# One-hot rows of destinations made by VectorE instead of ScalarE, and two of 128 gather groups loaded row by row from ScalarE's queue

## The chip, the cores and the metric

The kernel runs on one core of one Trainium2 chip. The metric is the device time of one execution in microseconds (us), lower is better. Five engines work side by side, each through its own queue in order: TensorE (PE; PEld is its weight loads), VectorE (DVE), ScalarE (ACT), GpSimd (POOL) and SyncE (SP). They wait for each other through semaphores. SP, ACT and POOL also issue DMA transfers.

## The reference

One graph attention layer with a residual and a layer norm. There are 12500 nodes of 96 features, 8 heads of 12, and 412500 edges, sorted by destination:

```
Q, K, V = x @ Wq + bq, x @ Wk + bk, x @ Wv + bv          # per node
E       = edge_attr @ We + be                            # per edge
score   = exp(clip(sum_head(K[src] * Q[dst] / sqrt(12) * E), -5, 5))
wV, Z   = segment_sum(V[src] * score, dst), segment_sum(score, dst)
out     = layernorm(x + wV / (Z + 1e-6))
```

## The kernel before

A first part of some 140 us makes a table of K and V rows and a table of Q rows in HBM, and works out for each chunk of edges its least destination. The main loop then goes over 806 chunks of 512 edges (128 partitions times 4 groups), one chunk a step, in loops unrolled by 32 steps. The last part, some 65 us, turns the sums back, divides, adds x and normalises. All order is written out by hand: each engine has its own list of instructions per step, and semaphores tie the lists.

What each engine does in one step s of the main loop:

- POOL gathers the K and V rows of a chunk's sources, one indirect DMA for each group of 128 edges (L683), into a ring of 16 slots. It may run up to eight chunks ahead of the messages that VectorE has made (the wait for `msg_ready`).
- SP loads edge attributes, query windows and destinations for eight chunks ahead. It also loads one group of one chunk in 32 by single rows.
- ACT waits for the scores of chunk s-1 and takes their exponential twice (L940, L942). Then it makes the one-hot rows `ohT` of chunk s+4 in two passes: `away` = abs(destination - row) (L946), `ohT` = relu(1 - away) (L949). Every fourth step it copies source numbers (L904). Then it loads single rows.
- PE projects the edge attributes (L798), picks the query rows with `ohT` (L803), sums the messages of chunk s-5 (L809) and transposes the edge attributes of chunk s+3 (L820).
- DVE adds the sums of chunk s-5 (L1156), multiplies keys, queries and edges (L1171, L1174), sums per head (L1178). Then it waits for the exponentials of chunk s-1, makes `oh` (L1183) and the messages (L1195). It copies the transposed edge attributes of chunk s+2 out of PSUM (L1202, `eaT`) and clips the scores of chunk s (L1209).

The single rows are in `load_rows`: with `load_row_sources` a list of source numbers (`act_idx`, `sp_idx`) is put on one partition. Then each step reads some entries of the list into registers with one TENSOR_LOAD (L466) and issues one small DMA for each entry (L470):

```
for p0 in range(first, last, ROW_LOAD):          # ROW_LOAD = 10
    count = min(ROW_LOAD, last - p0)
    nodes = nc.values_load_multi_w_load_instructions(idx[0:1, p0:p0 + count], ...)
    for r, node in zip(range(p0, p0 + count), nodes):
        engine.dma_start(rows[...], kv_dram[bass.ds(node, 1), :] ...)
```

ACT does this for one group of the chunk at place 31 of every 32: the list is asked for at place u = 0, and from u = 1 on five rows a step are issued (places 1 to 26). In a loaded step they stand in ACT's queue between the exponentials of one step and those of the next. SP issues 19 rows every four steps, as a list read of ten entries and one of nine.

Of the kernel before, what the change touches and what calls it, by code (L numbers as in the profile page):

```python
# [5 lines left out]
ALU = mybir.AluOpType  # L6
ACT = mybir.ActivationFunctionType
# [7 lines left out]
P = 128  # L15
HEADS = 8
G = 4
CHUNK = P * G
# [4 lines left out]
DEPTH = 4  # L23
TURN_LEAD = 3
COPY_LEAD = 2
Q_DEPTH = 2
TURN_DEPTH = 2
MSG_RING = 8
OUT_RING = 8
TURN_DST = 9  # L30
SEL = WIN * PARTS
SEL_READ = 106
SEL_LOAD = 102
RING = 16
KV_RING = 16
HALF = 4
# [4 lines left out]
BLOCK = 32  # L41
SP_CHUNK = 15
ACT_CHUNK = 31
ACT_GROUPS = 1
SP_STEP = 19
ACT_STEP = 5
ROW_LOAD = 10
IDX_RING = 16
IDX_GROUP = 4
# [39 lines left out]
def gnn_kernel(nc, x, src, dst, edge_attr, Wq, bq, Wk, bk, We, be, Wv, bv, out):  # L89
    N, D = x.shape  # L90
# [4 lines left out]
    C = (E + CHUNK - 1) // CHUNK  # L95
# [23 lines left out]
    with ExitStack() as ctx:  # L119
        def sb(name, shape, dt=F32):  # L120
            return ctx.enter_context(nc.sbuf_tensor(name, shape, dt))

        def sem(name):
            return ctx.enter_context(nc.semaphore(name))
# [7 lines left out]
        part = sb("part", [P, 1])  # L132
        sel_row_i = sb("sel_row_i", [P, 1], I32)
        sel_row = sb("sel_row", [P, 1])
        minus_row = sb("minus_row", [P, 1])
        ident = sb("ident", [P, P])
        w_kvq = sb("w_kvq", [DA, 3 * D])
        w_e = sb("w_e", [DA, D])
# [22 lines left out]
        accT = sb("accT", [P, N_PAD])  # L161
# [12 lines left out]
        most = sb("most", [1, 1], I32)  # L174
        act_idx = sb("act_idx", [1, ACT_GROUPS * P], I32)
        act_rows = sb("act_rows", [P, ACT_GROUPS, 2 * D])
        sp_idx = sb("sp_idx", [1, P], I32)
# [6 lines left out]
        off_b = off_mem[:, :].rearrange("p (c e) -> p c e", e=CHUNK)  # L184
# [4 lines left out]
        away = sb("away", [SEL, 2, CHUNK], BF16)  # L189
        ohT = sb("ohT", [SEL, MSG_RING, CHUNK], BF16)  # L190
# [14 lines left out]
        acc_first = sb("acc_first", [P, 1])  # L205
# [62 lines left out]
        off8_made = sem("off8_made")  # L268
        off8_stored = sem("off8_stored")
        tabs_in = sem("tabs_in")  # L270
        minus_row_set = sem("minus_row_set")
        node_id_ready = sem("node_id_ready")
        dst_turned = sem("dst_turned")
        rel_made = sem("rel_made")
# [1 line left out]
        acc_zeroed = sem("acc_zeroed")  # L276
# [7 lines left out]
        kv_in = [sem(f"kv_in{i}") for i in range(KV_RING)]  # L284
        act_idx_in = sem("act_idx_in")
        act_rows_allowed = sem("act_rows_allowed")
        act_rows_in = [sem(f"act_rows_in{i}") for i in range(2 * ACT_GROUPS)]
        sp_idx_in = sem("sp_idx_in")
        sp_rows_allowed = sem("sp_rows_allowed")
        sp_rows_in = [sem(f"sp_rows_in{i}") for i in range(2)]  # L290
# [1 line left out]
        columns_made = sem("columns_made")  # L292
        ea_flipped = sem("ea_flipped")
        ea_turned = sem("ea_turned")
        away_done = sem("away_done")
        ohT_built = sem("ohT_built")
        kq_done = sem("kq_done")
        kqe_done = sem("kqe_done")
# [53 lines left out]
        def landed_half(engine, c, u):  # L352

            if isinstance(c, int):
                engine.wait_ge(off_b_in[u // HALF], 16 * (c // RING + 1))
            else:
                engine.wait_ge(off_b_in[u // HALF], (c - u) * (16 // RING) + 16)
# [92 lines left out]
        WHOLE = C // BLOCK * BLOCK  # L450
        gathered = {SP_CHUNK: G - 1, ACT_CHUNK: G - ACT_GROUPS}

        def groups_gathered(s, u):

            return G if isinstance(s, int) and s == SP_CHUNK else gathered.get(u, G)
# [21 lines left out]
        block = ctx.enter_context(nc.Block())  # L477
# [397 lines left out]
        def _(act):  # L875
# [24 lines left out]
            def copy_sources(s, u):  # L900

                count = max(0, min(IDX_GROUP, C - s)) if isinstance(s, int) else IDX_GROUP
                if count > 0:
                    nc.scalar.copy(src_idx[:, u:u + count, :], src_tab[:, bass.ds(s * G, count * G)].rearrange(  # L904
                        "p (c g) -> p c g", g=G)).then_inc(src_copied, count)
# [22 lines left out]
            run_batches(act, query_batch, BATCHES, 2, 1)  # L928


            act.wait_ge(minus_row_set, 1)

            wait_all(act, kv_stored)

            def step(s, u, _):

                m, t, w = s - 1, s + DEPTH, (u + DEPTH) % RING
                if not isinstance(s, int) or 0 <= m < C:
                    act.wait_ge(score_ready, m + 1)
                    nc.scalar.activation(msg[:, (u - 1) % MSG_RING, :, D:DZ],  # L940
                                         score[:, (u - 1) % 2, :].rearrange("p (g h) -> p g h", g=G), ACT.Exp)
                    nc.scalar.activation(weight_ps[(u - 1) % DEPTH], score[:, (u - 1) % 2, :], ACT.Exp).then_inc(exp_done, 1)  # L942
                if not isinstance(s, int) or t < C:
                    if w % HALF == 0:
                        landed_half(act, t, w)
                    nc.scalar.activation(away[:, u % 2, :], off_b[0:SEL, w, :], ACT.Abs,  # L946
                                         bias=minus_row[0:SEL, 0:1]).then_inc(away_done, 1)
                    act.wait_ge(away_done, t + 1)
                    nc.scalar.activation(ohT[:, w % MSG_RING, :], away[:, u % 2, :], ACT.Relu, bias=1.0, scale=-1.0).then_inc(ohT_built, 1)  # L949
                    if isinstance(s, int) and s == -1:  # L950
                        nc.scalar.copy(accT[:, N // 2:N], acc_first[:, 0:1].to_broadcast((P, N - N // 2))).then_inc(acc_zeroed, 1)

                if u % IDX_GROUP == 0 and (not isinstance(s, int) or s > 0):
                    copy_sources(s + IDX_AHEAD, (u + IDX_AHEAD) % IDX_RING)
                if not isinstance(s, int) or 0 <= s < WHOLE:
                    first = s - u
                    if u == 0:
                        load_row_sources(act, first + ACT_CHUNK, ACT_GROUPS, act_idx, act_idx_in)
                    if u == 1:

                        act.wait_ge(act_idx_in, first // 2 + 16)
                        act.sem_inc(act_rows_allowed, 1)
                        if not isinstance(first, int) or first > 0:
                            act.wait_ge(msg_ready, first)
                        act.sem_inc(act_rows_allowed, 1)
                    lo, hi = (u - 1) * ACT_STEP, min(u * ACT_STEP, ACT_GROUPS * P)
                    if u >= 1 and lo < hi:
                        load_rows(act, lo, hi, act_idx, act_rows, act_rows_in)
# [39 lines left out]
        def _(dve):  # L1008
# [13 lines left out]
            nc.vector.tensor_scalar(sel_row_i[:, :], sel_row_i[:, :], 9, None, ALU.logical_shift_right).then_inc(ident_step, 1)  # L1022
            dve.wait_ge(ident_step, 3)
            nc.vector.tensor_copy(sel_row[:, :], sel_row_i[:, :]).then_inc(ident_step, 1)
            nc.vector.tensor_scalar(minus_row[:, :], sel_row_i[:, :], -1.0, None, ALU.mult).then_inc(minus_row_set, 1)
            nc.vector.tensor_tensor(ident[:, :], iota[:, :], part[:, 0:1].to_broadcast((P, P)), ALU.is_equal).then_inc(ident_ready, 1)
            dve.wait_ge(w_kvq_in, 16 * 6)
            nc.vector.tensor_scalar(w_kvq[:, 2 * D:3 * D], w_kvq[:, 2 * D:3 * D], QSCALE, None, ALU.mult).then_inc(w_q_scaled, 1)
# [94 lines left out]
            for b in range(BATCHES + 1):  # L1123
                query_batch(b, b % 4)
                k = b - BATCHES // 2
# [8 lines left out]
            def step(s, u, base):  # L1134


                a, m, n = s, s - 1, s - SUM_LAG
# [19 lines left out]
                if scores:  # L1157
                    here, block = groups_gathered(a, u), a // BLOCK if isinstance(a, int) else block_now[0]
                    if u in gathered:

                        before = 0 if u == SP_CHUNK else 16 * gathered[SP_CHUNK]
                        dve.wait_ge(kv_in[ua], block * (16 * sum(gathered.values())) + (before + 16 * gathered[u] + 16))
                    else:
                        landed(dve, kv_in, a, ua, 16 * G, u)
                    if here < G:
                        for rows_in in sp_rows_in if u == SP_CHUNK else act_rows_in:
                            dve.wait_ge(rows_in, block * (8 * P) + (0 if u == SP_CHUNK else 8 * P))
                        rows = sp_rows if u == SP_CHUNK else act_rows
                        nc.vector.tensor_tensor(kqe[:, here:G, :], rows[:, :, 0:D],
                                                q_ps[u % Q_DEPTH][:, here * D:G * D].rearrange("p (g d) -> p g d", g=G - here), ALU.mult)  # L1170
                    nc.vector.tensor_tensor(kqe[:, 0:here, :], kv[:, ua, 0:here, 0:D],  # L1171
                                            q_ps[u % Q_DEPTH][:, 0:here * D].rearrange("p (g d) -> p g d", g=here), ALU.mult).then_inc(kq_done, 1)
                    dve.wait_ge(kq_done, a + 1)
                    nc.vector.tensor_tensor(kqe[:, :, :], kqe[:, :, :],  # L1174
                                            e_ps[v].rearrange("p (g d) -> p g d", g=G), ALU.mult).then_inc(kqe_done, 1)
# [23 lines left out]
                k = s + COPY_LEAD  # L1199
                if not isinstance(s, int) or 0 <= k < C:  # L1200
                    dve.wait_ge(ea_flipped, k + 1)
                    nc.vector.tensor_copy(eaT[0:D, (u + COPY_LEAD) % DEPTH, :], turn_ps[(u + COPY_LEAD) % TURN_DEPTH][0:D, :]).then_inc(ea_turned, 1)  # L1202
                if isinstance(s, int) and s == -1:

                    nc.vector.memset(accT[0:D, 0:N // 2], 0.0)
                    nc.vector.memset(accT[D:P, 0:N // 2], 1e-6).then_inc(acc_zeroed, 1)
# [130 lines left out]
```

## Time and profile before

| | before |
|---|---|
| time, median of 3 runs | 4123.18 us (4119.38 to 4124.28) |
| the profiled execution: time, span | 4121.44 us, 4119.6 us |
| mean granted TensorE clock | 0.509 of full speed |
| busy share of the span: PE, PEld | 87%, 85% |
| busy share: DVE, ACT, POOL | 66%, 34%, 75% |

Busy time counts neither instructions of an engine's sequencer (register reads, waits) nor the issue of DMAs. An engine that is 34% busy can still have a full queue. The span runs from the first to the last instruction; 1.84 us of the execution's time lie outside it.

### The profile page before, as it was taken

The page shows a single profiled execution, that of the slowest core. Times are in us where ns is not written, and L with a number is a line of the kernel's source. Part 1 is how long each engine was busy: PE and PEld are TensorE (multiplying, and loading weights), DVE is VectorE, ACT ScalarE, POOL GpSimd, SP SyncE. Part 2 cuts the span into 40 slices and gives each one's busy share as a digit, 9 for nine tenths or more (in the row PEclk, how much of TensorE's full clock was granted, in tenths as well). Part 3 has the DMA queues.
Part 4 walks back from the last instruction along what each step waited for, and adds up shares of the span by engine and source line. Part 5 has one row for each costly group of instructions (what it writes and reads, how often), then busy time and mean ns, then how long its engine had stood idle before and what let it go on. Part 6 is the DMA issues. An engine that isn't in the chain of part 4 may idle for free.

```text
span 4119.6 us, 87353 instructions
## 1 busy us (share of the span) xinstructions
PE 3603.4 (87%) x20000; PEld 3508.7 (85%) x20001; DVE 2730.4 (66%) x6963; ACT 1402.6 (34%) x3656; POOL 3096.0 (75%) x3312
## 2 busy tenths in 40 slices
PE   7799988888888888888888888888888888888886
PEld 7799988888888888888888888888888888888885
DVE  4777766666666666666666666666666666666667
ACT  3433333333333333333333333333333333333335
POOL 8777777777777777777777777777777777777775
PEclk8555555555555555555555555555555555555555
DMA  8555545444454454444544454444544444444443
GB/s 269 165 142 144 144 136 140 134 133 135 133 141 133 133 138 139 133 133 135 141 134 133 134 139 136 133 134 135 141 133 133 136 141 133 134 135 134 141 124 112
DMA packets 409729, 574.44 MB, mean 139 GB/s; under 512 B 160715, under 2 KB 330476, under 8 KB 409268
## 3 DMA queue, kind: packets, MB, share of 16 engines
q0 software_dynamic: 154480, 316.87, 29.3%
q1 hardware_dynamic: 237361, 239.83, 19.3%
q10 hardware_dynamic: 17426, 13.83, 1.1%
q14 instruction: 446, 3.65, 0.3%
q8 instruction: 16, 0.26, 0.0%
HBM read 547.39 MB, written 22.87 MB: 138 GB/s over the span
## 4 chain that ended last, share of the span: by engine, by line
POOL 53%; issue 20%; DVE 7%; DMA 6%; PE 4%; ACTq 3%; ACT 2%; POOLq 1%; DVEq 1%
POOL kv_mem L683 53%; DMA kv_mem<-kv_table,src_idx 5%; ACTq L470 3%; DVE kqe L1174 1%; PE bank L798 1%; DVE kqe L1171 1%; PE bank L809 1%; DVE msg_mem L1195 1%; ACT away L946 1%; PE bank L820 1%; ACT ohT L949 1%; ACTq L466 1%; DVE eaT L1202 1%; DVE oh L1183 1%; DVE y_stats L1296 0%
## 5 line engine op out<-in xcount | busy, mean ns | idle before, releaser
L683 POOL DMA_INDIRECT kv_mem<-kv_table,src_idx x3175 | 3004.0, 946 | 978.9 <-issue 946.3
L798 PE MATMUL bank<-w_e,eaT 97*128 97x96 f32 x6448 | 1500.1, 414 | 1.9 <-DVE eaT L1202 1.9
L798 PEld LDWEIGHTS bank<-w_e,eaT 97*128 97x128 f32 x6448 | 1474.4, 334 | 10.7 <-DVE eaT L1202 2.1
L820 PE MATMUL bank<-ident,ea_mem 128*96 128x128 f32 x3224 | 868.8, 425 | 450.1 <-DVE eaT L1202 435.6
L809 PE MATMUL bank<-oh,msg_mem 128*104 128x32 f32 x6448 | 1257.9, 360 | 1.9 <-DVE msg_mem L1195 1.9
L809 PEld LDWEIGHTS bank<-oh,msg_mem 128*104 128x104 f32 x6448 | 1211.2, 293 | 2.2 <-DVE msg_mem L1195 2.2
L940 ACT ACTIVATE msg_mem<-score 128x32 f32<-128x32 f32 x806 | 184.8, 229 | 2596.4 <-DVE score L1209 1956.7
L820 PEld LDWEIGHTS bank<-ident,ea_mem 128*96 128x96 f32 x3224 | 569.3, 205 | 518.2 <-DVE eaT L1202 478.0
L1171 DVE TENSOR_TENSOR kqe<-kv_mem,bank 128x384 f32<-128x384 f32 (+1 forms) x806 | 439.6, 545 | 716.1 <-DMA kv_mem<-kv_table,src_idx 711.2
L946 ACT ACTIVATE away<-off_mem,minus_row 96x512 bf16<-96x512 uint8 x806 | 568.8, 706 | 1.9 <-issue 1.9
L1202 DVE COPY eaT<-bank 96x512 f32<-96x512 f32 x806 | 547.8, 680 | 1.5 <-PE bank L820 1.5
L949 ACT ACTIVATE ohT<-away 96x512 bf16<-96x512 bf16 x806 | 507.4, 630 | 25.5
L1156 DVE TENSOR_TENSOR accT<-bank,accT 104x32 f32 x806 | 154.9, 192 | 508.3 <-PE bank L809 305.0
L1174 DVE TENSOR_TENSOR kqe<-kqe,bank 128x384 f32<-128x384 f32 x806 | 446.3, 554 | 27.8
L1178 DVE TENSOR_REDUCE raw_score<-kqe 128x32 f32<-128x384 f32 x806 | 445.7, 553 | 27.8
L1195 DVE TENSOR_TENSOR msg_mem<-kv_mem,bank 128x384 f32<-128x384 f32 (+1 forms) x806 | 433.7, 538 | 0.0
L803 PE MATMUL bank<-q_win,ohT 96*128 96x96 bf16 x3224 | 425.3, 283 | 4.9 <-DMA q_win<-q_table 4.9
L803 PEld LDWEIGHTS bank<-q_win,ohT 96*128 96x128 bf16 x3224 | 414.6, 161 | 12.5 <-DMA q_win<-q_table 5.2
L1183 DVE TENSOR_TENSOR oh<-bank,rel 128x128 f32<-128x128 f32 x806 | 226.7, 281 | 26.2 <-ACT bank L942 24.7
L1209 DVE TENSOR_SCALAR score<-raw_score 128x32 f32<-128x32 f32 x806 | 174.4, 216 | 0.0
L942 ACT ACTIVATE bank<-score 128x32 f32<-128x32 f32 x806 | 147.3, 183 | 0.0
L767 PE MATMUL bank<-w_kvq,accT 97*125 97x96 f32 x200 | 38.3, 375 | 13.1 <-DVE msg_mem L1116 12.2
(102 smaller groups left out, 606.4 us busy)
## 6 DMA issues: line engine op xcount, KB each, us to landing
ea_mem<-in_edge_attr_dram SPq DMA_DIRECT2D x201, 768.0 KB
act_rows<-kv_table ACTq DMA_DIRECT2D x3200, 0.8 KB
kv_mem<-kv_table,src_idx POOLq DMA_INDIRECT x3175
sp_rows<-kv_table SPq DMA_DIRECT2D x3072, 0.8 KB
off_mem<-offset_by_chunk SPq DMA_DIRECT2D x201, 204.0 KB
q_win<-q_table SPq DMA_DIRECT2D x806, 19.9 KB
kv_table<-kv_mem SPq DMA_DIRECT2D x25, 336.0 KB
q_table<-msg_mem ACTq DMA_DIRECT2D x25, 252.0 KB
```

The source lines that it names most:

```text
L683: pool.indirect_dma_start(kv[:, slot, g, :], None, kv_dram[:, :], bass.IndirectOffsetOnAxis(ap=src_idx[:, u % IDX_RING, g:g + 1], axis=0)) ...
L798: nc.tensor.matmul(e_ps[v][:, g * D:(g + 1) * D], eaT[:, v, g * P:(g + 1) * P], w_e[:, :], start=True, stop=True)
L803: last = nc.tensor.matmul(q_ps[u % Q_DEPTH][:, g * D:(g + 1) * D], ohT[:, u % MSG_RING, g * P:(g + 1) * P], q_win[0:SEL, u, :], start=(g = ...
L809: last = nc.tensor.matmul(sums_of(s, v), msg[:, w, g, :], oh[:, w % DEPTH, g, :], start=(g == 0), stop=(g == G - 1), skip_group_check=True)
L820: last = nc.tensor.transpose(turn_ps[w % TURN_DEPTH][0:D, g * P:(g + 1) * P], ea[:, w, g, :], ident[:, :])
L946: nc.scalar.activation(away[:, u % 2, :], off_b[0:SEL, w, :], ACT.Abs, bias=minus_row[0:SEL, 0:1]).then_inc(away_done, 1)
L949: nc.scalar.activation(ohT[:, w % MSG_RING, :], away[:, u % 2, :], ACT.Relu, bias=1.0, scale=-1.0).then_inc(ohT_built, 1)
L1171: nc.vector.tensor_tensor(kqe[:, 0:here, :], kv[:, ua, 0:here, 0:D], q_ps[u % Q_DEPTH][:, 0:here * D].rearrange("p (g d) -> p g d", g=here ...
L1174: nc.vector.tensor_tensor(kqe[:, :, :], kqe[:, :, :], e_ps[v].rearrange("p (g d) -> p g d", g=G), ALU.mult).then_inc(kqe_done, 1)
L1178: nc.vector.tensor_reduce(raw_score[:, :], kqe[:, :, :].rearrange("p g (h d) -> p (g h) d", d=HD), AX_X, ALU.add).then_inc(heads_summed, 1)
L1195: nc.vector.tensor_tensor(msg[:, um % MSG_RING, 0:here, 0:D].rearrange("p g (h d) -> p g h d", d=HD), kv[:, um, 0:here, D:2 * D].rearrange ...
L1202: nc.vector.tensor_copy(eaT[0:D, (u + COPY_LEAD) % DEPTH, :], turn_ps[(u + COPY_LEAD) % TURN_DEPTH][0:D, :]).then_inc(ea_turned, 1)
```

## The change

The one-hot rows `ohT` move from ACT to DVE. DVE makes them of chunk s+2, right after the copy of `eaT`, by one comparison of the destinations (`off_b`, bytes in SBUF) with the partition's row number (`sel_row`, one number per partition in SBUF, spread over the row). `away` and its two semaphores go. ACT now loads two groups of the chunk at place 31 instead of one. So POOL issues 125 gathers per 32 chunks in place of 126, ACT's list has 256 entries instead of 128, and it issues nine rows a step instead of five (28 steps of nine and one of four, at places 1 to 29).

```diff
-ACT_GROUPS = 1
+ACT_GROUPS = 2
 SP_STEP = 19
-ACT_STEP = 5
+ACT_STEP = 9
...
-            act.wait_ge(minus_row_set, 1)
...
-                m, t, w = s - 1, s + DEPTH, (u + DEPTH) % RING
+                m = s - 1
...
-                if not isinstance(s, int) or t < C:
-                    if w % HALF == 0:
-                        landed_half(act, t, w)
-                    nc.scalar.activation(away[:, u % 2, :], off_b[0:SEL, w, :], ACT.Abs,
-                                         bias=minus_row[0:SEL, 0:1]).then_inc(away_done, 1)
-                    act.wait_ge(away_done, t + 1)
-                    nc.scalar.activation(ohT[:, w % MSG_RING, :], away[:, u % 2, :], ACT.Relu, bias=1.0, scale=-1.0).then_inc(ohT_built, 1)
...
-                            dve.wait_ge(rows_in, block * (8 * P) + (0 if u == SP_CHUNK else 8 * P))
+                            dve.wait_ge(rows_in, block * (8 * P) if u == SP_CHUNK else block * (16 * P) + 16 * P)
...
                     nc.vector.tensor_copy(eaT[0:D, (u + COPY_LEAD) % DEPTH, :], turn_ps[(u + COPY_LEAD) % TURN_DEPTH][0:D, :]).then_inc(ea_turned, 1)
+                if not isinstance(s, int) or 0 <= k < C:
+                    w = (u + COPY_LEAD) % RING
+                    if w % HALF == 0:
+                        landed_half(dve, k, w)
+                    nc.vector.tensor_tensor(ohT[:, w % MSG_RING, :], off_b[0:SEL, w, :], sel_row[0:SEL, 0:1].to_broadcast((SEL, CHUNK)),
+                                            ALU.is_equal).then_inc(ohT_built, 1)
```

The order of ACT's instructions in a loaded step of the main loop, before. `msg_mem` and `bank` on `score` are the two exponentials, TENSOR_LOAD reads the list, and each DMA loads one row:

```order
L940 ACTIVATE msg_mem<-score 128x4x8
L942 ACTIVATE bank<-score 128x32
L946 ACTIVATE away<-off_mem,minus_row 96x512
L948 REGISTER_ALU
L949 ACTIVATE ohT<-away 96x512
L466 TENSOR_LOAD act_idx
L470 ISA
L470 DMA act_rows<-kv_table 1x192
```

The last two rows stand there five times in each such step. The same place in the changed kernel, where lines have moved up by some numbers:

```order
L935 REGISTER_ALU
L936 ACTIVATE msg_mem<-score 128x4x8
L938 ACTIVATE bank<-score 128x32
L463 TENSOR_LOAD act_idx
L467 ISA
L467 DMA act_rows<-kv_table 1x192
```

The two passes between the exponentials and the list read are gone, and the last two rows stand there nine times. The exponentials of the next step still follow the last row's DMA.

The order of DVE's instructions in the second half of a step of the main loop, before:

```order
L1183 TENSOR_TENSOR oh<-bank,rel 128x128
L1195 TENSOR_TENSOR msg_mem<-kv_mem,bank 128x4x96
L1201 REGISTER_ALU
L1202 COPY eaT<-bank 96x512
L1209 TENSOR_SCALAR score<-raw_score 128x32
```

And in the changed kernel:

```order
L1171 TENSOR_TENSOR oh<-bank,rel 128x128
L1183 TENSOR_TENSOR msg_mem<-kv_mem,bank 128x4x96
L1189 REGISTER_ALU
L1190 COPY eaT<-bank 96x512
L1195 TENSOR_TENSOR ohT<-off_mem,sel_row 96x512
L1203 TENSOR_SCALAR score<-raw_score 128x32
```

The comparison stands between the copy of `eaT` and the clipping of the scores, which it pushes back. It is the only instruction of DVE's loop step whose two inputs both lie in SBUF.

## Rows read from the trace of the kernel before

**Rows 1.** The page: the span, and the costliest group of instructions.

```profile
span 4119.6 us, 87353 instructions
...
L683 POOL DMA_INDIRECT kv_mem<-kv_table,src_idx x3175 | 3004.0, 946 | 978.9 <-issue 946.3
```

**Rows 2.** Waits of POOL: total us, how many, the longest.

```profile
POOL kv_mem L683 <- issue: 946.3, 3088, 5.2
```

**Rows 3.** The gathers' line: ns min/median/max, first and last start in us.

```profile
L683 POOL DMA_INDIRECT kv_mem<-kv_table,src_idx x3175: 942/946/1305, 70.8 to 4046.3; - x199
```

**Rows 4.** Timeline of POOL, the last gathers: start, us, instruction, idle before.

```profile
4043.81 0.95 POOL L683 DMA_INDIRECT kv_mem<-kv_table,src_idx  x1 [0.30 <-issue]
4045.06 0.95 POOL L683 DMA_INDIRECT kv_mem<-kv_table,src_idx  x1 [0.30 <-issue]
```

**Rows 5.** Timeline of ACT, one loaded step up to the next, and a source copy.

```profile
2026.06 0.23 ACT L940 ACTIVATE msg_mem<-score 128x32 f32<-128x32 f32 x1 [3.42 <-DVE score L1209]
2026.20 0.18 ACT L942 ACTIVATE bank<-score 128x32 f32<-128x32 f32 x1
...
2027.06 0.63 ACT L949 ACTIVATE ohT<-away 96x512 bf16<-96x512 bf16 x1
2028.52 1.94 ACTq L470 DMA_DIRECT2D act_rows<-kv_table  x5
2030.51 0.23 ACT L940 ACTIVATE msg_mem<-score 128x32 f32<-128x32 f32 x1 [2.82 <-issue]
...
2036.48 0.19 ACT L904 CAST src_idx<-src_tab 128x16 int32 x1
```

**Rows 6.** List reads in four short windows: ns min/median/max, start in us.

```profile
L466 ACTq TENSOR_LOAD <-act_idx x1: 720/720/720, 2022.0 to 2022.0; - x1
L466 ACTq TENSOR_LOAD <-act_idx x1: 1300/1300/1300, 2027.1 to 2027.1; - x1
L466 SPq TENSOR_LOAD <-sp_idx x1: 1026/1026/1026, 1943.6 to 1943.6; - x1
L466 SPq TENSOR_LOAD <-sp_idx x1: 2142/2142/2142, 2002.6 to 2002.6; - x1
```

**Rows 7.** Row loads of ACT's queue in one loaded step, 2146.6 to 2149.

```profile
L470 ACTq DMA_DIRECT2D act_rows<-kv_table x5: 217/217/452, 2146.7 to 2148.5; - x5
```

**Rows 8.** Waits of ACT: total us, how many, the longest.

```profile
ACT msg_mem L940 <- issue: 639.7, 214, 5.4
```

**Rows 9.** Timeline of all engines in the first part, DVE and POOL rows.

```profile
85.89 0.55 DVE L1120 TENSOR_TENSOR msg_mem<-msg_mem 125x384 bf16<-125x384 f32 x1
85.98 1.28 POOL L683 DMA_INDIRECT kv_mem<-kv_table,src_idx  x1 [0.30 <-issue]
...
87.57 0.95 POOL L683 DMA_INDIRECT kv_mem<-kv_table,src_idx  x1 [0.30 <-issue]
...
88.02 0.55 DVE L1120 TENSOR_TENSOR msg_mem<-msg_mem 125x384 bf16<-125x384 f32 x1
```

**Rows 10.** Lines of DVE with two inputs in SBUF: ns min/median/max.

```profile
L1120 DVE TENSOR_TENSOR msg_mem<-msg_mem x25: 545/548/559, 68.6 to 122.6; 125x384 bf16<-125x384 f32 x25
L1088 DVE TENSOR_TENSOR rel<-rel,base_all x7: 628/629/636, 98.5 to 112.7; 128x460 int16<-128x460 int16 x6, 128x464 int16<-128x464 int16 x1
```

**Rows 11.** Timeline of DVE: the same instruction of two steps without waits between.

```profile
145.39 0.56 DVE L1171 TENSOR_TENSOR kqe<-kv_mem,bank 128x384 f32<-128x384 f32 x1
...
148.56 0.56 DVE L1171 TENSOR_TENSOR kqe<-kv_mem,bank 128x384 f32<-128x384 f32 x1
```

**Rows 12.** The chain that ended last, in order of time: start, us, what.

```profile
251.14 1.65 PE bank L798 x8
255.35 1.65 PE bank L798 x8
...
276.68 4.69 DMA act_idx<-in_src_dram
...
1977.00 1.85 DVEq L379
```

**Rows 13.** The exponentials' line: ns min/median/max, first and last start.

```profile
L940 ACT ACTIVATE msg_mem<-score x806: 229/229/232, 142.2 to 4051.6; 128x32 f32<-128x32 f32 x162
```

More of the change, by code:

```diff
@@ L134, in gnn_kernel @@
         sel_row = sb("sel_row", [P, 1])
-        minus_row = sb("minus_row", [P, 1])
         ident = sb("ident", [P, P])
@@ L270, in gnn_kernel @@
         tabs_in = sem("tabs_in")
-        minus_row_set = sem("minus_row_set")
         node_id_ready = sem("node_id_ready")
@@ L286, in gnn_kernel @@
         act_rows_allowed = sem("act_rows_allowed")
-        act_rows_in = [sem(f"act_rows_in{i}") for i in range(2 * ACT_GROUPS)]
+        act_rows_in = [sem(f"act_rows_in{i}") for i in range(2)]
         sp_idx_in = sem("sp_idx_in")
@@ L294, in gnn_kernel @@
         ea_turned = sem("ea_turned")
-        away_done = sem("away_done")
         ohT_built = sem("ohT_built")
@@ L942, in step @@
                     nc.scalar.activation(weight_ps[(u - 1) % DEPTH], score[:, (u - 1) % 2, :], ACT.Exp).then_inc(exp_done, 1)
-                if not isinstance(s, int) or t < C:
-                    if w % HALF == 0:
-                        landed_half(act, t, w)
-                    nc.scalar.activation(away[:, u % 2, :], off_b[0:SEL, w, :], ACT.Abs,
-                                         bias=minus_row[0:SEL, 0:1]).then_inc(away_done, 1)
-                    act.wait_ge(away_done, t + 1)
-                    nc.scalar.activation(ohT[:, w % MSG_RING, :], away[:, u % 2, :], ACT.Relu, bias=1.0, scale=-1.0).then_inc(ohT_built, 1)
-                    if isinstance(s, int) and s == -1:
-                        nc.scalar.copy(accT[:, N // 2:N], acc_first[:, 0:1].to_broadcast((P, N - N // 2))).then_inc(acc_zeroed, 1)
+                if isinstance(s, int) and s == -1:
+                    nc.scalar.copy(accT[:, N // 2:N], acc_first[:, 0:1].to_broadcast((P, N - N // 2))).then_inc(acc_zeroed, 1)
                 if u % IDX_GROUP == 0 and (not isinstance(s, int) or s > 0):
@@ L1024, in _ @@
             nc.vector.tensor_copy(sel_row[:, :], sel_row_i[:, :]).then_inc(ident_step, 1)
-            nc.vector.tensor_scalar(minus_row[:, :], sel_row_i[:, :], -1.0, None, ALU.mult).then_inc(minus_row_set, 1)
             nc.vector.tensor_tensor(ident[:, :], iota[:, :], part[:, 0:1].to_broadcast((P, P)), ALU.is_equal).then_inc(ident_ready, 1)
```

## The prediction

> **What bounds the kernel now.** The page comes first: the costliest group is POOL's gathers, 3004.0 us busy with 978.9 us of idle time in front of them, so 3983 of 4119.6 us are spent there [rows 1]. The waits of POOL say what that idle time is: 946.3 us of it in 3088 pieces is "issue", which means that POOL waited for nothing outside itself [rows 2]. The timeline shows the same to the last gather: one of 0.95 us starts every 1.25 us, with 0.30 us between [rows 4]. The line as a whole agrees: 3175 gathers from 70.8 to 4046.3 us are 1.25 us each [rows 3]. So POOL sets the pace: 126 gathers of 1.25 us are 157.5 us per 32 chunks, 4.92 us a chunk. Everything else has to fit under that, and what matters is by how much.
>
> PE is close below. Where the first part had let POOL run ahead, the chain of waits goes through PE, and its projection comes back after 255.35 - 251.14 = 4.21 us [rows 12]. DVE is further off: a step without a wait takes 148.56 - 145.39 = 3.17 us [rows 11], without the 0.1 us that adding the sums still costs there.
>
> ACT is 34% busy, but busy time leaves out its sequencer, so its timeline is read instead. In a loaded step the exponentials start at 2026.06; five row loads end at 2028.52 + 1.94 = 2030.46; the next exponentials start at 2030.51, and what held them is "issue", ACT's own queue [rows 5]. Such waits sum to 639.7 us in 214 places [rows 8]. A loaded step therefore takes ACT 4.45 us, whatever DVE does. That is below 4.92, so it costs nothing now. Next to it is where I expect the change to be decided.
>
> **The change part by part.**
>
> *One gather in 126 goes.* 25 blocks of 32 chunks times 1.25 us [rows 4] are 31.3 us, if POOL stays the bound. That is all that the change can win: 4121.4 - 31.3 = 4090.1.
>
> *The two passes on ACT go.* With five rows the list read began with the second pass, 2027.06 - 2026.06 = 1.00 us after the exponentials [rows 5, 6]. Now it can begin with the second exponential, 2026.20 - 2026.06 = 0.14 us after them. That gives back 0.86 us a step.
>
> *Nine rows a step instead of five.* Two things grow. The first is the row loads: of the 1.94 us of five, the first takes 0.45 [rows 5, 7], so each further one takes (1.94 - 0.45) / 4 = 0.37 us, and four more 1.49. The second is the list read, and its rows need care. ACT's read of five entries takes 0.72 or 1.30 us, SP's of nine 1.03 or 2.14 us [rows 6]. I counted places from the start of the block: the two short reads begin at entries 40 and 48 of the list, the long ones at 45 and 105. So a read is short where it begins at a multiple of four. A list read nine at a time begins at 0, 9, 18 and so on: of 28 reads of nine, 7 begin at a multiple of four and 21 don't. No row shows ACT reading nine. The bounds are ACT's five entries (1.30 and 0.72) and SP's nine (2.14 and 1.03), and I take SP's, since the count is the same.
>
> The loaded step of ACT is then: 0.14 to the list read; the read; and what followed it with five rows, 2030.51 - (2027.06 + 1.30) = 2.15 us [rows 5, 6], plus 1.49, so 3.64. With a long read 0.14 + 2.14 + 3.64 = 5.92 us, with a short one 4.81. Seven of the long steps also copy sources (0.19 us [rows 5], of which I count 0.12, since activations overlap). The 28 steps take 21 x 5.92 + 7 x 4.81 + 7 x 0.12 = 158.8 us. This is not hidden by anything. The exponentials of the next step stand behind the row loads in the same queue, DVE waits for them before it makes messages, and its scores, for which ACT waits in turn, come later in the same step. One chunk per ACT step is all that gets through.
>
> The four steps without a full load go at the pace of what is next. Three of them take PE's 4.21 us [rows 12]. The fourth is place 0, where DVE reads eight window numbers in 1.85 us [rows 12]: 3.17 + 0.1 + 1.85 + 0.6 for the comparison (below) = 5.72. Together 18.4 us, and 177.2 for a block, where POOL needs 125 x 1.25 = 156.3. POOL will run its eight chunks ahead and wait.
>
> *The list is twice as long.* With 128 entries it landed after 4.69 us in one block of the chain [rows 12]. It is asked for at place 0 and needed about 5.3 us later, so it is still in time if it lands as before (nothing). If it takes twice as long, 9.4 us, each block grows by 4 us, 100 in all. I take nothing, since one transfer of tiny pieces over many engines need not double.
>
> *The comparison on DVE.* The nearest rows with two inputs in SBUF are 548 ns for 384 elements and 629 ns for 460 [rows 10]; on that line 512 elements take 0.68 us. Neighbours overlap by some 0.08, so 0.6 us a step. DVE then needs 3.9 us of a step, under 4.21 and 5.92, and in loaded steps it waits for ACT anyway: nothing. TensorE still gets `ohT` two steps ahead.
>
> *What the comparison does to POOL.* One gather of the first part started at 85.98 and took 1.28 us instead of 0.95, while an instruction of DVE with two inputs in SBUF ran from 85.89 to 86.44; the gather from 87.57 was as short as ever, though another such instruction began at 88.02, in its middle [rows 9]. So a gather seems to be held if such an instruction runs at a point soon after its start, until that instruction ends: 86.44 less the 0.33 lost puts the point 0.13 us after the start. With no phase preferred, a comparison of 0.68 us covers that point in 0.68 / 1.25 of the cases and holds for half of 0.68 then: 0.185 us a chunk, 149 us over 806 chunks. It lies between 0 (never met) and 0.68 a chunk (always met at once). Here it is covered by ACT: 32 x 0.185 = 5.9 us bring POOL's block to 162, still under 177.
>
> [...]
>
> *The sum.* The first exponential is at 142.2 us, and the span ends 4119.6 - 4051.6 = 68.0 us after the last [rows 1, 13]. Between them now stand 25 blocks of 177.2 and five steps of 4.21: 142.2 + 4430 + 21 + 68.0 = 4661. With 1.8 us outside the span, and some more for row loads slower than the one measured, I say 4670 us, against 4121.4 of the profiled execution (1.7 below the median of the runs shown).
>
> **The rivals.**
>
> *ACT does not bind, POOL is held by the comparison.* For it: only SP shows a read of nine. If ACT's take 1.30 us and 0.72, the loaded steps take 5.08 and 4.50 and a block 21 x 5.08 + 7 x 4.50 + 0.8 + 18.4 = 157.4, less than POOL's 162. Against it: ACT's reads of five fall into the same two kinds as SP's of nine. The time would be 4121.4 - 31.3 + 149 = 4239; with the bound of 0.68 a chunk, 4638.
>
> [...]
>
> *Faster: POOL stays the bound and is not held.* ACT's loaded step would have to stay under (156.3 - 18.4) / 28 = 4.92 us on average; mine is 5.67. That needs long list reads that take as little as the short ones, and a comparison that never meets a gather's point: DVE starts on landed gathers, so its phase could settle in a free place. Then 4090.
>
> *Slower still.* A list that lands late (plus 100) or rows that take longer with both queues issuing: 0.04 us more on nine rows of 28 x 25 steps is 250 us.
>
> **How the numbers follow.** ACT's queue decides, as worked out: 0.80. POOL held: 0.12, of which whole exclusion 0.02. Faster by the gathers alone: 0.03; within 0.2%, about what a measurement of this kernel can tell from no change: 0.01. Above the range: 0.04. The range goes from 4560 to 4790: below, some list reads shorter than SP's; above, the late list. That leaves out POOL held and the ends, 2 in 10. Slower by over 0.2%: 0.96.
>
> **What the profile after would show.** If I am right, ACT's list reads have a median near 2.1 us, loaded steps lie 5.9 and 4.8 us apart, POOL's idle time has a large new part that waits for messages of DVE, and DVE waits for the exponentials more than for gathers. Gathers in the main loop that take over 0.95 us show the comparison's hold. I am wrong if POOL's idle time stays "issue" to the end: then the list reads will be short, and the mean gather tells which rival it is.

## The result, and the profile after

The changed kernel takes 4666.53 us (median of 4 runs, 4661.98 to 4697.72) against 4122.85 us before: a ratio of 1.134, with a 95% interval of 1.129 to 1.139. The prediction was 4670.

The page of the changed kernel: the span, the chain that ended last by engine and by line, and the group of the gathers.

```profile
span 4660.2 us, 96080 instructions
...
ACTq 44%; issue 41%; DVE 4%; ACT 4%; DMA 3%; DVEq 0%; POOL 0%; POOLq 0%
ACTq L467 42%; DMA act_idx<-in_src_dram 3%; ACT msg_mem L936 3%; ACTq L463 2%; DVE ohT L1195 1%; ACT bank L938 1%; DVE eaT L1190 1%; DVE msg_mem L1183 1%; DVE kqe L1162 0%; ACTq L935 0%; DVE y_stats L1290 0%; DVE oh L1171 0%; DVE kqe L1159 0%; DVEq L376 0%; DVE score L1203 0%
...
L680 POOL DMA_INDIRECT kv_mem<-kv_table,src_idx x3150 | 3109.1, 987 | 1392.5 <-issue 925.3
```

POOL has left the chain. In its place stands ACT's sequencer (ACTq): the row loads (L467, which was L470) and "issue", the time of register reads in which an engine waits for nothing that the profile shows. ACT's busy share fell to 8%, and yet its queue is what the kernel waits for.

The waits of POOL, ACT and DVE, three views of the changed kernel in one fence: total us, how many, the longest.

```profile
POOL kv_mem L680 <- DVE msg_mem L1183: 461.1, 414, 9.4
...
ACT msg_mem L936 <- issue: 3734.7, 700, 6.3
...
DVE oh L1171 <- ACT bank L938: 853.1, 577, 2.3
```

These are links of one chain. ACT's exponentials waited for ACT's own queue in 700 places, 28 a block in 25 blocks; before it was 214 [rows 8]. DVE waited for them before `oh`, and POOL, its chunks ahead used up, waited for DVE's messages.

ACT's timeline shows three loaded steps of the changed kernel.

```profile
2000.86 0.23 ACT L936 ACTIVATE msg_mem<-score 128x32 f32<-128x32 f32 x1 [5.48 <-issue]
...
2003.30 3.40 ACTq L467 DMA_DIRECT2D act_rows<-kv_table  x9
2006.81 0.23 ACT L936 ACTIVATE msg_mem<-score 128x32 f32<-128x32 f32 x1 [5.51 <-issue]
...
2008.00 3.70 ACTq L467 DMA_DIRECT2D act_rows<-kv_table  x9
2011.81 0.23 ACT L936 ACTIVATE msg_mem<-score 128x32 f32<-128x32 f32 x1 [4.68 <-issue]
...
2014.17 3.41 ACTq L467 DMA_DIRECT2D act_rows<-kv_table  x9
2017.69 0.23 ACT L936 ACTIVATE msg_mem<-score 128x32 f32<-128x32 f32 x1 [5.57 <-issue]
```

The steps take 5.95, 5.00 and 5.88 us, where the five-row step took 4.45 [rows 5]. The list reads of the first two, in short windows, and of all 725, with the first and last exponentials:

```profile
L463 ACTq TENSOR_LOAD <-act_idx x1: 2127/2127/2127, 2001.0 to 2001.0; - x1
...
L463 ACTq TENSOR_LOAD <-act_idx x1: 987/987/987, 2006.9 to 2006.9; - x1
...
L463 ACTq TENSOR_LOAD <-act_idx x725: 493/2141/2300, 143.3 to 4555.0; - x182
...
L936 ACT ACTIVATE msg_mem<-score x806: 229/229/231, 143.1 to 4592.1; 128x32 f32<-128x32 f32 x162
```

The median read of ACT takes 2141 ns, as SP's did before [rows 6]. From the first to the last exponential it is 4449 us; less five steps of 4.21, a block of 32 chunks takes 177.1 us.

### The profile page after: what moved, and what is told of

Its sections match the earlier page's. It is cut to its first block, busy times and chain, and to the rows that moved or that the text cites. A ratio compares the mean times of both kernels' runs of the same rounds, so it can differ in the third digit from the quotient of the medians.

```text
span 4660.2 us, 96080 instructions
## 1 busy us (share of the span) xinstructions
PE 3670.9 (79%) x20000; PEld 3531.8 (76%) x20001; DVE 3197.7 (69%) x7768; ACT 383.8 (8%) x2044; POOL 3201.1 (69%) x3287
## 4 chain that ended last, share of the span: by engine, by line
ACTq 44%; issue 41%; DVE 4%; ACT 4%; DMA 3%; DVEq 0%; POOL 0%; POOLq 0%
ACTq L467 42%; DMA act_idx<-in_src_dram 3%; ACT msg_mem L936 3%; ACTq L463 2%; DVE ohT L1195 1%; ACT bank L938 1%; DVE eaT L1190 1%; DVE msg_mem L1183 1%; DVE kqe L1162 0%; ACTq L935 0%; DVE y_stats L1290 0%; DVE oh L1171 0%; DVE kqe L1159 0%; DVEq L376 0%; DVE score L1203 0%
## 5 line engine op out<-in xcount | busy, mean ns | idle before, releaser
L680 POOL DMA_INDIRECT kv_mem<-kv_table,src_idx x3150 | 3109.1, 987 | 1392.5 <-issue 925.3
L817 PEld LDWEIGHTS bank<-ident,ea_mem 128*96 128x96 f32 x3224 | 529.8, 192 | 1038.9 <-DVE eaT L1190 996.8
L1195 DVE TENSOR_TENSOR ohT<-off_mem,sel_row 96x512 bf16<-96x512 uint8 x806 | 546.5, 678 | 0.0
L1159 DVE TENSOR_TENSOR kqe<-kv_mem,bank 128x384 f32<-128x384 f32 (+2 forms) x806 | 431.8, 536 | 5.2 <-issue 4.9
L1183 DVE TENSOR_TENSOR msg_mem<-kv_mem,bank 128x384 f32<-128x384 f32 (+2 forms) x806 | 431.4, 535 | 2.3
L1203 DVE TENSOR_SCALAR score<-raw_score 128x32 f32<-128x32 f32 x806 | 143.2, 178 | 0.0
L703 POOL TENSOR_TENSOR kv_mem<-kv_mem,x_res 125x384 f32<-125x384 f32 x25 | 25.0, 1000 | 48.4 <-DVE kv_mem L1284 48.4
```

The source lines that it names most:

```text
L680: pool.indirect_dma_start(kv[:, slot, g, :], None, kv_dram[:, :], bass.IndirectOffsetOnAxis(ap=src_idx[:, u % IDX_RING, g:g + 1], axis=0)) ...
L817: last = nc.tensor.transpose(turn_ps[w % TURN_DEPTH][0:D, g * P:(g + 1) * P], ea[:, w, g, :], ident[:, :])
L1183: nc.vector.tensor_tensor(msg[:, um % MSG_RING, 0:here, 0:D].rearrange("p g (h d) -> p g h d", d=HD), kv[:, um, 0:here, D:2 * D].rearrange ...
L1195: nc.vector.tensor_tensor(ohT[:, w % MSG_RING, :], off_b[0:SEL, w, :], sel_row[0:SEL, 0:1].to_broadcast((SEL, CHUNK)), ALU.is_equal).then_ ...
```

## The experiments

The theory is that ACT's queue sets the pace of the changed kernel, through row loads and long list reads, and that the comparison holds gathers besides, hidden under ACT. Rival A: the hold of the gathers is the cause. Rival B: the comparison costs POOL nothing. Rival C: the number of rows counts, and where a list read begins doesn't matter. "Of before" is against the kernel before, timed along with each batch of runs: at 4120.53 us for the first four (e1 to e4), 4123.98 for the next three (e5 to e7), 4119.70 for the last two (e8, e9).

**The comparison alone** (e1). VectorE makes the one-hot rows, ACT loads one group.

```diff
-ACT_GROUPS = 2
+ACT_GROUPS = 1
...
-ACT_STEP = 9
+ACT_STEP = 5
...
```

> The one-hot rows by the comparison on VectorE, as in the change, but ScalarE loads one group with five rows a step, as before. Theory (ScalarE's queue sets the pace of the changed kernel): here its loaded step falls to 0.14 + 1.30 + 2.15 = 3.6 us, under POOL's 4.92, so POOL is the bound again with 3175 gathers; it loses only what the comparison holds up, 131 us in the trace of the changed kernel: a span of about 4250 us, mean gather near 987 ns. Rival A (the hold of the gathers is what slowed the change): about 4660. Rival B (the comparison costs nothing to POOL): 4120.

4192.21 us, 1.0178 of before (1.0161 to 1.0195). The page's group of the gathers, with all releasers:

```profile
L680 POOL DMA_INDIRECT kv_mem<-kv_table,src_idx x3175 | 3080.5, 970 | 974.3 <-issue 928.5 <-DVE msg_mem L1183 39.0 <-DMA kv_table<-kv_mem 6.8
```

POOL is the bound again, so rival A falls: without the row loads most of the loss is gone. Rival B falls too: gathers take 970 ns on average instead of 946 [rows 1], 24 ns x 3175 = 76 us, and the time is 72 us longer. The hold is real, but smaller than the 131 us of the changed kernel that the expectation carried over, so the time is 58 us under the 4250 expected.

The timeline of e1 shows one gather held and its neighbour free:

```profile
2009.22 0.68 DVE L1195 TENSOR_TENSOR ohT<-off_mem,sel_row 96x512 bf16<-96x512 uint8 x1
2009.52 1.21 POOL L680 DMA_INDIRECT kv_mem<-kv_table,src_idx  x1 [0.30 <-issue]
2011.03 0.95 POOL L680 DMA_INDIRECT kv_mem<-kv_table,src_idx  x1 [0.30 <-issue]
```

The comparison ends at 2009.90, 0.38 us after the gather's start, and the gather is 0.26 longer than its neighbour: it was held from 0.12 us after its start, the point that the first part of the kernel before had shown [rows 9].

Running at that point is not enough, though. Here the comparison began 0.02 us before the gather and ran far past the point:

```profile
2879.91 0.75 DVE L1195 TENSOR_TENSOR ohT<-off_mem,sel_row 96x512 bf16<-96x512 uint8 x1
2879.93 0.95 POOL L680 DMA_INDIRECT kv_mem<-kv_table,src_idx  x1 [0.30 <-issue]
```

The gather kept its 0.95 us, and the comparison took 0.75 instead of 0.68. Counted over the traces, of the comparisons that began 0.54 to 0.04 us before a gather, 290 of 292 held it in e1 and 520 of 520 in the changed kernel (a gather of over 0.96 us counts as held). Of those that began between 0.03 us before and 0.125 us after its start, none did, 0 of 38 and 0 of 23.

**The loads alone** (e2). From the kernel before: the two passes stay on ACT.

```diff
-ACT_GROUPS = 1
+ACT_GROUPS = 2
...
-ACT_STEP = 5
+ACT_STEP = 9
...
```

> The two passes stay on ScalarE as before the change; only the loads change: two groups, nine rows a step. Theory: the 0.86 us a step of the two passes come back into ScalarE's queue, 28 steps take 158.8 + 24 = 183 us, a block 201, the span 142 + 25 x 201 + 21 + 68 = 5256 us; gathers stay at 946 ns. Rival A (the hold is the cause): no comparison, no hold, about 4090.

5280.25 us in one run, 24 more than expected. What ACT no longer does in the changed kernel (the passes) had given back about 610 us, and the nine rows had cost more than that.

```profile
L683 POOL DMA_INDIRECT kv_mem<-kv_table,src_idx x3150 | 2978.4, 946 | 2146.1 <-DVE msg_mem L1195 1220.6 <-issue 905.3 <-ACT src_idx L904 13.9
```

The gathers are back at 946 ns, and POOL waits 1220.6 us for messages. So the longest of these kernels is one without any hold.

**List reads that begin at multiples of four** (e3). The changed kernel with the same rows per block.

```diff
-ACT_STEP = 9
...
+ACT_ENDS = [0]
+for u in range(1, 30):
+    ACT_ENDS.append(ACT_ENDS[-1] + (4 if u == 29 else 12 if u % 4 == 2 else 8))
...
-                        load_rows(act, lo, hi, act_idx, act_rows, act_rows_in)
+                        load_rows(act, ACT_ENDS[u - 1], ACT_ENDS[u], act_idx, act_rows, act_rows_in, 12)
```

> The changed kernel with the same 256 rows per 32 chunks in the same places (28 steps and one of four), but cut as 8, 12, 8, 8 rows instead of 9, so that every list read begins at a multiple of four. Theory: reads of 8 take about 0.72 us and of 12 about 1.2, loaded steps 4.13 and 6.1, a block 21 x 4.21 + 7 x 6.1 + 18.4 = 150 us, so POOL is the bound again with 125 gathers and the hold: about 4121 - 31 + 131 = 4221 us. Rival C (the number of rows sets it, the place where a read begins doesn't matter): as the changed kernel, 4660.

4192.60 us, 1.0176 of before (1.0159 to 1.0193): 474 us less than the changed kernel with the same number of rows. It is 28 us under the expectation: the hold came out as 30 ns x 3150 = 94 us, not as 131.

**The same list, one entry further** (e4). Only the address of the list differs from e3.

```diff
-        act_idx = sb("act_idx", [1, ACT_GROUPS * P], I32)
+        act_idx_mem = sb("act_idx", [1, 1 + ACT_GROUPS * P], I32)
+        act_idx = act_idx_mem[:, 1:1 + ACT_GROUPS * P]
```

> The kernel whose reads begin at multiples of four, with the whole list put one entry further, so that none of its reads does; nothing else differs. Theory: reads of 8 take about 1.93 us and of 12 about 2.77 (0.21 us an entry, from 1.30 for five and 2.14 for nine), loaded steps 5.34 and 7.66, a block 21 x 5.34 + 7 x 7.66 + 18.4 = 184 us, the span 142 + 25 x 184 + 21 + 68 = 4834. Rival C: no difference from the kernel with reads at multiples of four.

4896.34 us in one run, 704 more than e3; 62 more than expected. ACT's list reads in e3 and in e4, ns min/median/max:

```profile
L465 ACTq TENSOR_LOAD <-act_idx x725: 480/724/1018, 138.6 to 4072.9; - x182
```

```profile
L466 ACTq TENSOR_LOAD <-act_idx x725: 1082/1941/2861, 141.8 to 4789.6; - x182
```

This decides against rival C: four bytes of address make the median read of eight entries 1941 ns instead of 724. The reads of twelve are the longest in both, some 0.96 and 2.78 us. In sum the 28 reads grow by 21 x 1.22 + 7 x 1.8 = 38 us a block. The time grew by 704 / 25 = 28, so ACT's slack in e3 hides the rest.

**The row number in PSUM** (e5). The changed kernel, with one input of the comparison moved.

```diff
+        sel_ps = [q_ps[i][:, 511:512] for i in range(Q_DEPTH)]
...
+            for i in range(Q_DEPTH):
+                nc.vector.tensor_copy(sel_ps[i], sel_row[:, :]).then_inc(sel_made, 1)
...
-                    nc.vector.tensor_tensor(ohT[:, w % MSG_RING, :], off_b[0:SEL, w, :], sel_row[0:SEL, 0:1].to_broadcast((SEL, CHUNK)),
+                    nc.vector.tensor_tensor(ohT[:, w % MSG_RING, :], off_b[0:SEL, w, :], sel_ps[u % Q_DEPTH][0:SEL, 0:1].to_broadcast((SEL, CHUNK)),
...
```

> The changed kernel with one difference: the row number that the comparison reads lies in PSUM instead of SBUF, so that VectorE has one input in SBUF. ScalarE's nine rows stay. Theory (ScalarE's queue sets the pace): the gathers go back to 946 ns, and the span stays at 4660 us within 10, since POOL has to wait anyway. Rival A (the hold of the gathers is the cause): at least the 131 us of hold are gone, 4530 or less.

4680.33 us, 1.1349 of before (1.1332 to 1.1367). That is not shorter than the changed kernel; the two intervals overlap. It is 10 us outside what was expected.

```profile
L682 POOL DMA_INDIRECT kv_mem<-kv_table,src_idx x3150 | 2983.0, 947 | 1536.0 <-issue 912.2 <-DVE msg_mem L1188 617.3 <-DMA kv_table<-kv_mem 6.5
```

The hold is gone (947 ns), and POOL's waits for messages grew from 461.1 to 617.3 us instead. So the hold was hidden in the changed kernel, as the prediction had it.

**Comparison alone, row number in PSUM** (e7). The edits of e1 and e5.

> The comparison on VectorE with its row number in PSUM; ScalarE loads one group with five rows a step, as before the change. Theory: POOL is the bound with 3175 gathers of 946 ns, as before: 4120 us within 5. With the row number in SBUF the same kernel should take about 130 us longer. If the hold comes from VectorE being busier, and not from the second input in SBUF, the two take the same.

4122.92 us, 0.9996 of before (0.9987 to 1.0005), with gathers of 948 ns on average. Against e1 this is the second input in SBUF alone: some 70 us. The 0.6 us a step that VectorE has more to do costs nothing, so a busier VectorE is not what holds the gathers.

**Both mended** (e6). The edits of e3 and e5.

> Both mended: list reads begin at multiples of four (8, 12, 8, 8 rows a step), and the comparison's row number lies in PSUM. Theory: neither ScalarE's queue nor the comparison holds POOL, one gather in 126 is gone: 4121 - 31 = 4090 us, ratio to before 0.992. If the hold has another cause than the second input in SBUF: about 4221, as with the row number in SBUF.

4110.08 us, 0.9965 of before (0.9951 to 0.9978). That is below the kernel before by more than the interval, but 20 us above the expectation. The waits of POOL between 260 and 450 us show where most of that went:

```profile
POOL kv_mem L684 <- DVE msg_mem L1189: 17.1, 13, 4.7
```

Pieces of 0.30 us are the plain gap between gathers, so 17.1 - 13 x 0.3 = 13 us are lost there, and none after (75 pieces, the longest 0.3). In that stretch the other engines still catch up with POOL, at 148 to 150 us a block (from the starts of the exponentials), and the lead that the kernel allows POOL shrinks from 16 chunks at the start to the 8 of the rest.

**Room for sixteen chunks** (e8). Added to e6:

```diff
-                room = max(KV_RING // 2, KV_RING - max(0, s - KV_RING) // 6) if isinstance(s, int) else KV_RING // 2
+                room = KV_RING
```

> The kernel with both mended (reads at multiples of four, row number in PSUM), and POOL allowed to run 16 chunks ahead instead of 8 once the ring is in use. Its trace with 8 shows POOL waiting for messages 13 us in all between 270 and 440 us, while the other engines take 148 to 150 us a block there, and never after. Theory: those waits are what keeps it from 4090: with 16 about 4091 us. Rival: the gathers' own time or the tail is what is missing, then 4104 as with 8.

4091.34 us, 0.9935 of before (0.9922 to 0.9949). With this the rival falls, and the change collects most of what one gather in 126 is worth: 4119.70 - 4091.34 = 28 of the 31 us.

**One input and a number per partition** (e9). The edits of e3, and the comparison in another form.

```diff
-                    nc.vector.tensor_tensor(ohT[:, w % MSG_RING, :], off_b[0:SEL, w, :], sel_row[0:SEL, 0:1].to_broadcast((SEL, CHUNK)),
-                                            ALU.is_equal).then_inc(ohT_built, 1)
+                    nc.vector.tensor_scalar(ohT[:, w % MSG_RING, :], off_b[0:SEL, w, :], sel_row[0:SEL, 0:1], None, ALU.is_equal).then_inc(ohT_built, 1)
```

> The kernel whose reads begin at multiples of four (row number in SBUF, POOL 8 chunks ahead), with the comparison written as an operation on one input and a number per partition, in place of two inputs. Theory (a second input stream in SBUF is what holds the gathers): no hold, gathers at 946 ns, about 4104 us as with the row number in PSUM; the comparison may also get shorter. Rival: any read of the row number from SBUF holds them: about 4185, as with two inputs.

4128.01 us, 1.0019 of before (1.0009 to 1.0028), between the two expectations.

```profile
L1196 DVE TENSOR_SCALAR ohT<-off_mem,sel_row x806: 471/473/722, 124.4 to 4044.7; 96x512 bf16<-96x512 uint8 x162
```

The comparison gets shorter, 473 ns instead of 677, but now it is stretched itself at times, to 722. What the gathers took over 946 ns each sums to 25 us (mean 953 ns), against 96 in e3. So "a second input stream" is too narrow a cause. The trace shows a second place besides: 78 gathers were held by a comparison that began 0.35 to 0.5 us after their start, and all 159 comparisons that began 0.5 to 0.7 us after one's start were stretched. What in this form does it was not tried.

## Why the prediction was right

*ACT's loaded steps.* 5.92 and 4.81 us were predicted; 5.88 (5.95 with a source copy) and 5.00 came. Both list reads were right to 0.05 us, so SP's reads of nine were the right rows to take. In the step with the short read above, the rows themselves took 3.70 us instead of 3.40; the cause of that is open.

*The block.* 177.2 us predicted, 177.1 measured, and the span 4660.2 against a sum of 4661. That is closer than the terms deserve, and in part luck, since two errors of under 1 us a block cancel. One is the late list (below). The other is the four steps without a full load, at 18.4: in the block that ends at 2092.71 the exponentials of places 29 to 1 start 2.64, 3.87, 4.70 and 6.83 us apart, less while DVE catches up, more at place 0, and 18.0 in sum.

*The list of twice the length.* It was taken to land in time. It came later than the 4.69 us of [rows 12], by these rows of the chain, in order of time:

```profile
2086.20 7.40 DMA act_idx<-in_src_dram
2093.80 0.98 ACTq L463
```

The packets themselves took no longer: in the DMA records of ACT's queue the load of [rows 12] is 144 packets of 4 bytes from 278.45 to 280.89, up to seven at the same time, and this one 258 from 2090.63 to 2092.73, up to four. They began 4.43 us after the issue instead of 1.77. It landed at 2093.60 and the read began at 2093.80, where ACT could have begun at about 2092.85. So it costs some 0.9 us in this block. Over the 25 blocks the first reads began some 18 us too late in sum, between the predicted nothing and the bound of 100.

*The comparison.* 0.68 us predicted, 677 ns measured, and hidden as said. Its hold on POOL was put at 0.185 us a chunk; it was 129 / 806 = 0.16 in the changed kernel and 76 / 806 = 0.09 in e1. The step that failed there is that every comparison which covers the point holds the gather: those that begin with the gather or after it hold nothing (the counts under e1), and they were the ones priced with the longest holds. Without them the window is 0.68 - 0.13 - 0.03 = 0.52 us and the mean hold half of that, so with no phase preferred an estimate is 0.52 / 1.25 x 0.26 = 0.11 us a chunk. The rest is phase, which differs between the kernels: 292 of 806 comparisons began in the window counted under e1 there, and 520 in the changed kernel. Why the phase falls so was not tried.

*The rivals.* "POOL held" is real where ACT's queue is taken away: e3, with the rows and gathers of the change, takes 4192 us, where 4239 was priced. Whole exclusion, given 0.02, would mean that neither a comparison nor a gather runs while the other does. No run shows it: in the changed kernel DVE sat idle for 0.0 us before its 806 comparisons, and the longest took 754 ns, 77 more than the median, where a gather takes 946. "Faster by the gathers alone" needed exactly the two conditions named, short list reads and no hold, and with them it came: 14 us in e6, and 28 once POOL was also let run further ahead (e8).

## What to carry to other kernels

Work moved off an engine frees only the part of its queue that it held: the two passes gave ACT back about 610 us (e2 against the changed kernel), and its loaded step still grew from 4.45 to 5.88 us. So read an engine's step in its timeline from one instruction to the same one a step later, register reads and DMA issues included, and hold it against the pace of the bound. When a kernel is bound by gathers of POOL, look at the operands of what is put beside them, not only at its duration: the same comparison cost 70 us (e1) or nothing (e7), by where one small number lay. A lead that one engine may take over others has to last until the others have caught up: with 16 chunks instead of 8 the kernel took 19 us less (e8 against e6).

## What the runs showed of the hardware

ACT's list reads (one TENSOR_LOAD of consecutive 4-byte entries in SBUF) took less where they began at a multiple of four entries of the list. There it read 5 entries in 0.72 us [rows 6], 8 in 0.72 (e3) and 9 in 0.99 (changed kernel). Elsewhere they took 1.30 [rows 6], 1.94 (e4) and 2.13 us (changed kernel). A shift of the list by one entry cost 704 us of a whole kernel (e4 against e3).

POOL's gathers were held beside the comparison with two inputs in SBUF. In e1 and the changed kernel, of the comparisons that began 0.54 to 0.04 us before a gather, 810 of 812 held it. The gather was then longer than 946 ns by the time from a point 0.112 to 0.130 us after its start to the comparison's end. Of the 61 comparisons that began between 0.03 us before and 0.125 us after a gather's start none held it. Close to that start they were lengthened themselves instead, by up to 77 ns (754 against 677, changed kernel). With the row number in PSUM (e5) 608 comparisons began in the first of these windows, and no gather of theirs took over 0.96 us; the mean gather took 947 ns. With one input and a number per partition (e9) the mean gather took 953 ns, against 976 in e3, and the comparison up to 722 ns against a median of 473.
